# Last unit's values placed behind the next group's first scores, and the narrow units of the second attention placed between wide ones

## The reference

```
x = x + attn_a(layernorm(x))   # 32 heads of 16, rotary positions, all keys
x = x + ffn(layernorm(x))      # x @ W.T + bias + mean over 8 low-rank pairs
x = x + attn_b(layernorm(x))   # 32 heads of 16, ALiBi bias, causal
x = x + ffn(layernorm(x))
```

## Time and profile before

| | |
|---|---|
| time, median of 3 runs | 1784.81 us (1781.09 to 1786.96) |
| the profiled execution's own time | 1787.05 us |
| its span | 1785.2 us |
| first attention, first to last exponential | 206.5 to 882.2 us |
| second attention, first to last exponential | 1185.3 to 1650.5 us |
| PE busy | 1646.3 us, 92% |
| DVE busy | 1393.8 us, 78% |
| ACT busy | 971.8 us, 54% |
| mean granted TensorE clock | 0.967 |

### The profile page before, as it was taken

One profiled execution on the slowest core, in us unless ns is written; L12 is line 12 of the kernel. 1 busy time (PEld: TensorE's weight loads), 2 busy tenths in 40 slices (PEclk: granted clock), 3 DMA queues, 4 the chain that ended last, 5 costly groups with the idle time before them and its releaser, 6 DMA issues. The chain is left out here.

```text
span 1785.2 us, 32918 instructions
## 1 busy us (share of the span) xinstructions
PE 1646.3 (92%) x13040; PEld 849.3 (48%) x13040; DVE 1393.8 (78%) x3007; ACT 971.8 (54%) x1103; POOL 138.6 (8%) x216
## 2 busy tenths in 40 slices
PE   6898999999999999999879999899999999999598
PEld 3554333333333333333335777555454545454476
DVE  3766799999999999999366364568888888885486
ACT  3432277777777777777711112126666666667110
POOL 3332200000000000000000011010000000003000
PEclk9999699999999999999999999989999999999799
DMA  7766334333333332330260433663636363632311
GB/s 217 226 165 193 81 56 85 63 62 64 60 63 65 55 55 56 56 55 12 86 196 1 141 116 104 202 155 57 118 73 103 65 109 60 108 61 63 103 71 71
DMA packets 116801, 167.58 MB, mean 94 GB/s; under 512 B 20772, under 2 KB 58036, under 8 KB 116532
## 3 DMA queue, kind: packets, MB, share of 16 engines
q1 hardware_dynamic: 115176, 160.99, 39.1%
q0 software_dynamic: 1472, 4.49, 1.3%
HBM read 100.41 MB, written 64.50 MB: 92 GB/s over the span
## 5 line engine op out<-in xcount | busy, mean ns | idle before, releaser
L356 DVE TENSOR_REDUCE mxp<-ps_m 128x1 f32<-128x512 f32 x1280 | 799.3, 684 | 69.3 <-PE ps_m L322 63.6
L673 ACT ACTIVATE a_p<-a_ps_s 128x1024 f32<-128x1024 f32 x512 | 522.2, 1025 | 149.8 <-PE a_ps_s L594 138.4
L673 ACT ACTIVATE b_p<-b_ps_s 128x1024 f32<-128x1024 f32 (+1 forms) x320 | 294.7, 938 | 157.9 <-PE b_ps_s L594 154.6
L353 DVE CUSTOM_DVE_ANT_0 ps_m<-ps_m,b_masks 128x128 f32<-128x128 f32 (+3 forms) x512 | 240.1, 517 | 45.1 <-PE ps_m L322 40.9
L322 PE MATMUL ps_m<-slot_qk 62*128 62x512 f32 (+3 forms) x624 | 230.7, 451 | 12.4 <-DVE mxp L356 9.0
L322 PE MATMUL ps_m<-a_slot_qk 62*128 62x512 f32 x640 | 238.1, 450 | 0.8
L594 PE MATMUL a_ps_s<-a_slot_qk 64*128 64x512 f32 x640 | 232.2, 443 | 1.3
L618 PE MATMUL a_ps_o<-a_p,a_slot_v 128*32 128x256 f32 x2560 | 205.6, 390 | 10.0 <-ACT a_p L673 5.4
L594 PEld LDWEIGHTS a_ps_s<-a_slot_qk 64*128 64x128 f32 x640 | 96.2, 185 | 128.8 <-issue 122.7
L594 PE MATMUL a_ps_s<-slot_qk 64*128 64x512 f32 x384 | 136.3, 455 | 0.6
L618 PE MATMUL a_ps_o<-a_p,slot_memory 128*32 128x256 f32 x1536 | 124.3, 393 | 7.4 <-ACT a_p L673 3.3
(11 more groups left out here) (205 smaller groups left out, 2343.7 us busy)
## 6 DMA issues: line engine op xcount, KB each, us to landing
va_groups<-w_o SPq DMA_DIRECT2D x16, 512.0 KB, 3.7
ka_parts<-pa_parts SPq DMA_DIRECT2D x16, 512.0 KB, 3.8
qa_parts<-pa_parts SPq DMA_DIRECT2D x32, 256.0 KB, 3.7
kb_parts<-slot_memory SPq DMA_DIRECT2D x16, 512.0 KB, 4.1
qb_parts<-slot_memory SPq DMA_DIRECT2D x32, 256.0 KB, 3.8
vb_groups<-w_proj SPq DMA_DIRECT2D x16, 512.0 KB, 3.4
a_slot_qk<-qa_parts SPq DMA_DIRECT2D x60, 128.0 KB, 4.1
a_slot_qk<-ka_parts SPq DMA_DIRECT2D x48, 128.0 KB, 6.3
```

The costliest lines, as they stand in the source:

```text
L353: dve.tensor_tensor_reduce(from_, from_, mask_of_query[:, CHUNK - keys:], 1.0, LOWEST, ALU.add, ALU.max, accum_out=to).then_inc(piece_take ...
L356: dve.tensor_reduce(to, from_, AX.X, ALU.max).then_inc(piece_taken, 1)
L673: act.activation(p_sb[:, (2 * u + pair) % NP, :, off:CHUNK], ps_s[:, 2 * pair:2 * pair + 2, off:CHUNK], ACT.Exp, scale=scale).then_inc(exp ...
```

## The change

The two parts of the last unit's values no longer end a step: they stand in the next step, behind the first and the second half unit of its unit 0, where other units have the values of the unit before. ACT's copy of the second half moves from a step's end to behind unit 0's exponentials of the next step. The last group's values and copy come after the loop. This holds for both attentions. In the second attention, units 3 to 9 (wide, wide, wide, wide, wide, narrow, narrow: kt 0, 1, 2, 3, 4, 5, 6 with 7) become kt 0, 1, 5, 2, 6 with 7, 3, 4: wide, wide, narrow, wide, narrow, wide, wide. No instruction is added or taken away.

```diff
@@ units
-        for kt in range(last - (2 if causal else 0)):
-            units.append((qh, [block(qh, kt)]))
+        own = [(qh, [block(qh, kt)]) for kt in range(last - (2 if causal else 0))]
         if causal:
             (_, _, _, at), (kt, off, n, _) = wide, narrow = block(qh, last - 2), block(qh, last - 1)
-            units.append((qh, [wide, (kt, off, n, at - n)]))
+            own.append((qh, [wide, (kt, off, n, at - n)]))
+        if causal and qh:
+
+            full, part = own[:-2], own[-2:]
+            own = full[:2] + part[:1] + full[2:3] + part[1:] + full[3:]
+        units += own
@@ PE
+                def values_behind(s, u, part):
+
+                    if u:
+                        values(s, s % SLOTS, u - 1, part)
+                    elif s:
+                        values(s - 1, (s - 1) % SLOTS, NU - 1, part)
+
@@ PE, step
                         half_unit(s, j, u, 0, lo, cut)
-                        if u:
-                            values(s, j, u - 1, 0)
+                        values_behind(s, u, 0)
                         half_unit(s, j, u, 1, cut, hi)
-                        if u:
-                            values(s, j, u - 1, 1)
-                    values(s, j, NU - 1, 0)
-                    values(s, j, NU - 1, 1)
+                        values_behind(s, u, 1)
@@ PE, behind all steps
+                for part in range(2):
+                    values_behind(NG, 0, part)
@@ ACT, step
                         if u == last_of[0] + 1:
                             copy_out(s, 0)
-                    copy_out(s, 1)
+                        if u == 0 and s:
+                            copy_out(s - 1, 1)
@@ ACT, behind all steps
+                copy_out(NG - 1, 1)
```

## The result

The changed kernel takes 1817.35 us (median of 4 runs, 1809.85 to 1820.19), the kernel before it on the same chip 1784.47 (4 runs). The ratio is 1.0179, with a 95% interval of 1.0142 to 1.0216: slower by some 33 us, and outside the predicted range. The profiled execution took 1819.41.

What follows compares the result with a forecast made beforehand. PE and DVE were both nearly full in the first attention, PE's order deciding; in the second, the chain beside PE at a group's start mattered more. Terms -12.9 and +14.1 came to +1.2: 1786 us, range 1770 to 1801.

Steps and rivals of the forecast that it cites:

- First attention, -12.9: Group boundaries of the first attention: 0.52 us lost instead of 1.38, gaining 0.86 at each of 15 boundaries.
- Units 3 and 4, 6.05: Second attention, units 3 and 4 and what leads to unit 5: unchanged at 6.05 us a group.
- From unit 0 to unit 3, 9.75: Second attention, unit 0's first matmul to unit 3's scores: 9.75 us instead of 7.73, PE waiting 0.5 for shift rows.
- The wait of the turn for POOL: Second attention, group start: POOL ends at T + 1.65, so the turn goes at T + 1.75 instead of 1.35.
- a landing at 1371.6: Shift rows' arrival by the skill page's 2.0 us fixed DMA cost: 0.4 later than forecast, sum 6 us higher.
- The chain through SP: SP's queue, second attention: store ahead of shift takes 2.46 us, shift 2.25 more, so rows arrive at T + 9.75.
- Units 5 to 9, 14.3: Second attention, units 5 to 9 in the new order: 14.3 us a group instead of 15.52.
- the upper end of that step, 14.9: Units 5 to 9 of the second attention: 14.9 us if each wait for DVE is 0.3 longer.
- My second rival: PE at unit 3's scores: shift rows land later than packets show, 1.5 us per 0.1, 1 us giving 1801; chance 0.24.
- Nobody waited: Shift rows before the change: no wait for them, so landing up to 4.5 us after issue was not ruled out.
- The ends: Second attention: group 0 -1.2; last group +3.6 at unit 3 and about +0.5 for the wide last unit.
- slower at 0.32: Whole kernel: chance 0.32 of slower, from late shift rows and a first-attention boundary winning only half of 0.86.

Runs made afterwards that it cites:

- early values and the old order: Narrow units' values earlier (one-block: next unit's first half; two-block: both halves), against the deferred, old-order kernel with shift rows ahead of the store: 1803.29 us, ratio 1.0109.
- shift first, old order: Against the changed kernel: SP's shift rows ahead of the old group's store, units in the old order, deferral in both attentions kept; 1764.62 us, ratio 0.9882.

## Why the prediction was wrong

- **First attention, -12.9: right.** 12.5 less, groups of 41.6, and alone it gives 1770. Pricing the new boundary by the middle of the same group was exact to 0.03 us a boundary.
- **Units 3 and 4, 6.05: right** (6.06). **From unit 0 to unit 3, 9.75: right** (9.76), but by luck, as three terms were off and cancelled: the turn came at T + 1.48 (forecast 1.75), unit 0's values at T + 4.76 (5.1), and the rows took 2.65 from the issue instead of 2.25. The wait of the turn for POOL that I had forecast does not show. The Trainium skill ("DMA: Bandwidth & Descriptors", anatomy of one DMA) gives 2.0 us of fixed cost, for DMAs that GpSimd issues; the estimate from it was a landing at 1371.6, 2.64 after the first issue. The trace agrees for these two that SP issues (2.61 to 2.65), and the end of the packets, by which I went, was 0.4 early. The chain through SP was the right place. What I mis-sized there is what lies without it: by PE alone unit 3 comes at T + 8.87 and not 9.25, so the wait was 0.89 and not 0.5, and taking it away was worth more than I had thought.
- **Units 5 to 9, 14.3: mis-sized; this is the first step that failed.** 15.28, so 0.98 x 14 = 13.7 us more. Unit 5 was right (2.61 for 2.62); the others are longer by 0.26, 0.19, 0.15 and 0.40. I had built each from pieces of the old units, and the upper end of that step, 14.9, was too low. The comparison that was missing is the old order with the deferral, where the same stretch takes 14.48. Against it my 14.3 was a gain of 0.2 by the new order; it is a loss of 0.80.
- **The clock: not in the sum at all; this is the second step that failed.** Four groups with it take 35.85, 36.17, 34.82 and 35.47 instead of 31.07, together 18.0 us, and two more, with a late SP, about 1.3. Of the 18.0, 5.2 is the longer wait itself (2.31, 2.19, 2.09 and 1.81 us instead of 0.79) and some 13 what the lower clock cost. My second rival had the place (PE at unit 3's scores, 1.5 us for each 0.1) but not the cause: the rows did not land late behind their issue (2.61 to 2.65 in every group), they were issued late, as SP's stores took longer. It also had no consequence of the wait for PE's clock. In the trace before I could have seen that SP's four stores take different times (from the store of a first half to the shift behind it mostly 2.5 us, but 3.35 to 3.72 in four groups), and that the clock at 1180 us falls while PE waits.
- **"Nobody waited" was a wrong reading of the trace before.** One group has a wait for these rows, 5.15 us behind the shift's issue at 1250.96, and is 0.6 us longer for it. I had taken 4.5 us as the most:

```profile
1256.11 0.50 PE L594 MATMUL b_ps_s<-slot_qk 64*128 64x512 f32 x1 [0.55 <-DMA slot_qk<-cturned]
```

- **The ends: nearly right.** Counted by T, unit 0's first matmul, the start (first exponential to the T of group 1) went from 33.11 to 31.86, -1.25 (forecast -1.2), and the last group (T to the last exponential) from 21.24 to 24.53, +3.3 (forecast +4.1).

The sum again, by profile, with a group counted from T to T: 14 x 1.77 = 24.8 for the groups, 18.3 for the four with the lower clock, 1.3 for those with a late SP alone, less 0.6 for the one of before that was long, 2.0 for the ends: 45.8, measured 45.9. With -12.5 it is 33.4, measured 32.4 between the spans. Of the gap between forecast and result, 31 us, 14 are units 5 to 9 and 18 the four groups in which the clock fell; the smaller terms come to -1 together.

The chances had slower at 0.32. The rival named for it had the right place, but its range ended at 1801 because each rival was priced alone. A late chain that also lowers the clock, and an order that is worse by its own, add up.

## What to carry to other kernels

A step deferred on one engine drags its DMA behind it: look at what stands after that DMA in the same queue, and put first what the next work waits for (some 27 us here). Where work is put into another order, price the order by itself against the old one with everything else already changed. A wait that turns up once in a round and differs from round to round should be priced by its longest, since a long wait of PE can take the clock with it.

## What the hardware showed that I had not expected

In the changed kernel the granted clock falls for 7 to 10 us in four of fifteen groups, each time within 2 us of the end of a wait of 1.81 to 2.31 us (2.09 at 1350.88); in other groups waits of 0.80, and one of 1.83, changed nothing. The Trainium skill ("TensorE: Matmul & The Clock Gate", on HAM oscillation) tells of waits for a DMA that bring the clock down again in every round; by that page such a wait costs more than itself. The trace agrees on the cost, 34.82 to 36.17 us for a group instead of 31.07, and not on every round. Dummy work in the gap kept the clock at 1.00.

It is not the whole rule. With early values and the old order the clock fell once without any wait for a DMA, when the longest wait of PE that the timeline shows just before it was 0.33 us:

```profile
1600.00:1605.00 5.00, 4.57 (x46) 2.35 (x43) 4.09 (x16) 2.54 (x3) 0.42 (x2) 0.91 0.00 0
1605.00:1610.00 5.00, 5.00 (x41) 2.99 (x40) 2.60 (x8) 2.32 (x3) 0.00 (x0) 0.50 0.05 13
```

It stayed at 0.50 for some 20 us, and this group took 36.81 instead of 30.48. What set it off was not tried and stays open. The runs of that kernel differ by 20 us from one to the next, those of the kernel whose profiled execution keeps its clock (shift first, old order) by 6.
